# Seven step inputs of a selective state-space recurrence on GpSimd, with their decays in PSUM

## The reference, cut to what matters

```
dt = softplus(dt_low @ dt_proj_w.T + dt_proj_b)          # [B, L, 256]
A  = -exp(A_log)                                         # [256, 16]
def step(h, t):
    dA = exp(dt_t[..., None] * A)                        # decay
    h  = dA * h + (dt_t * u_t)[..., None] * B_t[:, None, :]   # step input
    y_t = einsum('bdn,bn->bd', h, C_t)
y = y + u * D;  y = y * silu(z);  out = (y @ out_proj_w.T) @ fc2_w.T + fc2_b
```

## Time and profile before

| | |
|---|---|
| time, median of 3 runs | 1123.55 us (1122.48 to 1123.56) |
| profiled execution: its time, its span | 1121.12 us, 1119.8 us |
| TensorE busy | 1066.3 us (95%), granted clock 0.991 of full speed |
| VectorE, ScalarE, GpSimd busy | 839.1, 630.4, 763.4 us |
| the recurrence: first to last scan | 790.5 to 1018.9 us |
| the chain that ended last | PE 79%, issue 7%, DVE 6%, POOL 4%, ACT 3% |

### The profile page before, as it was taken

One profiled execution on the slowest core, in us unless ns is written; L12 is line 12 of the kernel. 1 busy time (PEld: TensorE's weight loads), 2 busy tenths in 40 slices (PEclk: granted clock), 3 DMA queues, 4 the chain that ended last, 5 costly groups with the idle time before them and its releaser, 6 DMA issues.

```text
span 1119.8 us, 18526 instructions
## 1 busy us (share of the span) xinstructions
PE 1066.3 (95%) x6860; PEld 662.1 (59%) x6860; DVE 839.1 (75%) x1234; ACT 630.4 (56%) x898; POOL 763.4 (68%) x394
## 2 busy tenths in 40 slices
PE   7999999999999999999999999779789987999998
PEld 4555665665665655665665657767344433446786
DVE  6876976776765775766975748235999999997987
ACT  5554655654644654643554635348986646757663
POOL 5788788787787897877899830230789897994200
PEclk9999999999999999999999999889899999999999
DMA  7000000000000000000000253465565443440000
GB/s 213 1 2 2 1 2 1 2 2 1 2 2 2 1 1 2 2 2 1 6 7 6 77 178 94 136 215 151 182 206 165 143 161 132 147 154 20 10 10 19
DMA packets 55369, 68.91 MB, mean 62 GB/s; under 512 B 23248, under 2 KB 41424, under 8 KB 55280
## 3 DMA queue, kind: packets, MB, share of 16 engines
q1 hardware_dynamic: 52272, 64.65, 18.7%
q0 software_dynamic: 1024, 2.10, 0.6%
q10 hardware_dynamic: 1984, 0.98, 0.3%
HBM read 61.30 MB, written 6.16 MB: 60 GB/s over the span
## 4 chain that ended last, share of the span: by engine, by line
PE 79%; issue 7%; DVE 6%; POOL 4%; ACT 3%; DMA 1%; another core or an unknown queue 1%; POOLq 0%; DVEq 0%; ACTq 0%
PE psum L661 20%; PE psum L622 16%; PE psum L647 6%; PE psum L635 5%; PE psum L1046 3%; PE psum L687 3%; PE psum L952 3%; PE psum L1029 3%; POOL hc L2252 3%; PE psum L746 3%; PE psum L702 2%; PE psum L810 2%; PE psum L821 2%; PE psum L726 2%; PE psum L680 2%
## 5 line engine op out<-in xcount | busy, mean ns | idle before, releaser
L2164 POOL TENSOR_TENSOR psums<-psums,prob 128x1024 f32<-128x1024 f32 x180 | 430.5, 2392 | 26.1 <-POOL psums L2164 0.5
L1627 DVE TENSOR_REDUCE mx<-psum 128x2 f32<-128x1024 f32 x256 | 299.8, 1218 | 102.0 <-PE psum L647 101.6
L1158 ACT ACTIVATE prob<-psum 128x1024 f32<-128x1024 f32 x256 | 261.3, 1026 | 62.6 <-PE psum L635 38.1
L661 PE MATMUL psum<-prob,V 128*64 128x512 f32 x1024 | 238.7, 597 | 0.0
L2252 POOL TENSOR_TENSOR hc<-hs,cc 128x1024 f32<-128x1024 f32 x64 | 151.6, 2368 | 21.1 <-DVE hs L1930 18.6
L1930 DVE TENSOR_TENSOR_SCAN hs<-dA,psum 128x1024 f32<-128x1024 f32 x64 | 146.3, 2287 | 2.2
L661 PEld LDWEIGHTS psum<-prob,V 128*64 128x64 f32 x1024 | 67.7, 137 | 106.7 <-issue 105.0
L2164 POOL TENSOR_TENSOR psums<-prob 128x1024 f32<-128x1024 f32 x30 | 72.1, 2403 | 85.0 <-ACT prob L1158 84.2
L1177 ACT COPY oraw<-psum 128x512 f32<-128x512 f32 x32 | 18.8, 587 | 191.3 <-PE psum L661 191.3
L952 PE MATMUL psum<-hc,ident 128*128 128x512 f32 x256 | 122.5, 601 | 2.8 <-DVE slot_rows_h L1938 1.4
L647 PE MATMUL psum<-k_hi,q_hi 64*128 64x512 f32 x512 | 107.0, 409 | 1.7 <-DVE mx L1627 1.3
(11 more groups left out here) (319 smaller groups left out, 1712.6 us busy)
## 6 DMA issues: line engine op xcount, KB each, us to landing
cc<-C_rows SPq DMA_DIRECT2D x64, 512.0 KB, 3.8
kq_wts<-in_e_rows SPq DMA_DIRECT2D x14, 578.0 KB, 4.2
e_wts<-in_e_rows SPq DMA_DIRECT2D x10, 578.0 KB, 3.9
e_w<-in_e_rows SPq DMA_DIRECT2D x6, 578.0 KB, 5.1
slots_in<-e_zero SPq DMA_DIRECT2D x2, 960.0 KB, 7.1
inv<-sum_rows SPq DMA_DIRECT2D x120, 1.0 KB, 2.0
slots_out<-e_y SPq DMA_DIRECT2D x30, 64.0 KB, 1.8
e_w<-in_e_w SPq DMA_DIRECT2D x1, 1024.0 KB, 7.0
```

Source lines behind the costliest of these rows:

```text
L661: ins = pe.matmul(A.O[HALF[s], :], A.V[pair % 2][:, j, s * DH:(s + 1) * DH], A.prob[unit(pair, c, j) % NPB][:, s * CH:(s + 1) * CH], start ...
L1158: act.activation(A.prob[n % NPB][:, :], slots.bank("score", pair, c, j).rearrange("p s n -> p (s n)"), ACT.Exp, scale=float(DH) ** -0.5).t ...
L1627: dve.tensor_reduce(K.A.mx[:, :, t, c], slots.bank("max", pair, t, c), AXX, ALU.max).then_inc(*slots.inc("max", pair, t, c))
L2164: pool.tensor_tensor(total[:, :], (K.A.prob[(n - 1) % NPB] if j == 1 else total)[:, :], K.A.prob[n % NPB][:, :], ALU.add).then_inc(*K.psum ...
```

## The change

Seven units, 19, 24, 27, 38, 43, 59 and 62 (`POOL_GAINS`), get their step input from GpSimd. For these units:

- SP stores the rows of B beside those of C in DRAM and loads row n of B into all partitions of one of two SBUF buffers (`sp_copy_B`), six units ahead or at unit 15. The buffers are halves of tiles that are free by then: the second half of xrows and of xnT. TensorE spreads no B.
- GpSimd multiplies that buffer by du in place (`pool_gain`), right behind the product of unit u - 3.
- ScalarE writes the decay into the PSUM buffer in which the step input would have stood (`decay_of`). It therefore waits for the scan of unit u - 2, no longer u - 3.
- The scan reads its decay from PSUM and its step input from SBUF.

GpSimd's side work moves: the bias of fc2 for batch 0 goes from unit 21 to ahead of the recurrence; the low parts of w1 stand at units 47, 49, ... 59 instead of 47 to 54; those of w2 at units 60 to 63 and behind the last unit instead of 56 to 63. Three semaphores of GpSimd's clearing at the start are merged into one.

```diff
+W1_LOW = {e: 45 + 2 * e for e in range(1, E1)}
+POOL_GAINS = (19, 24, 27, 38, 43, 59, 62)
+GAIN_AHEAD = 3
+B_FROM = 15
+def copied_at(i):
+    return max(B_FROM, POOL_GAINS[i] - 6, POOL_GAINS[i - 2] + 1 if i >= 2 else 0)
...
     for e in range(E1):
-        one[48 + e - 1] = one.get(48 + e - 1, []) + [("w1hi", e), ("w1lo", e)] * (e > 0)
-        one[56 + e] = [("w2hi", e), ("w2lo", e)]
+        one[48 + e - 1] = one.get(48 + e - 1, []) + [("w1hi", e)] * (e > 0)
+        one[56 + e] = [("w2hi", e)] + [("w2lo", e - 4)] * (e >= 4)
+    for e in range(1, E1):
+        one[W1_LOW[e]] += [("w1lo", e)]
...
+        order += [("w2lo", n + 2)] * (n + 2 < E1)
...
 def pe_spread_B(K, pe, u):
...
+    if u in POOL_GAINS:
+        return
...
+def decay_of(X, u):
+    return X.gain[u % 2] if u in POOL_GAINS else X.dA[u % 3][:, :]
...
 def act_decay(K, act, u):
...
-    if u >= 3:
+    if u in POOL_GAINS:
+        act.wait_ge(X.state_done, u - 1)
+    elif u >= 3:
         act.wait_ge(X.state_done, u - 2)
-    act.activation(X.dA[u % 3][:, :], X.dt[b][:, k, :], ACT.Exp, scale=X.alog[:, k, n:n + 1]).then_inc(X.decay_done, 1)
+    act.activation(decay_of(X, u), X.dt[b][:, k, :], ACT.Exp, scale=X.alog[:, k, n:n + 1]).then_inc(X.decay_done, 1)
...
 def dve_unit(K, dve, u):
...
+    gain = X.gain[u % 2]
+    if u in POOL_GAINS:
+        gain = X.B_copy[POOL_GAINS.index(u) % 2]
+    else:
+        dve.wait_ge(X.B_done, gains_by_dve(u))
...
+        dve.tensor_tensor(gain, gain, (X.du if u else X.dt)[b][:, k, :], ALU.mult).then_inc(X.gain_done, 1)
...
-    dve.tensor_tensor_scan(X.hs[u % 3][:, :], X.dA[u % 3][:, :], X.gain[u % 2], 0.0, ALU.mult, ALU.add).then_inc(X.state_done, 1)
+    dve.tensor_tensor_scan(X.hs[u % 3][:, :], decay_of(X, u), gain, 0.0, ALU.mult, ALU.add).then_inc(X.state_done, 1)
...
+def pool_gain(K, pool, u):
+    X = K.X
+    b, k, n = rec(u)
+    i = POOL_GAINS.index(u)
+    pool.wait_ge(X.du_done, KI * b + k + 1)
+    pool.wait_ge(X.B_copied[i % 2], 16 * (i // 2 + 1))
+    pool.tensor_tensor(X.B_copy[i % 2], X.B_copy[i % 2], X.du[b][:, k, :], ALU.mult).then_inc(X.pool_gained, 1)
...
 def pool_unit(K, pool, u):
...
+    if u + GAIN_AHEAD in POOL_GAINS:
+        pool_gain(K, pool, u + GAIN_AHEAD)
...
-    sp.dma_start(X.C_rows[b, :, :], X.xd[DTR + NS:DTR + 2 * NS, :]).then_inc(X.C_stored, 16)
+    sp.dma_start(X.C_rows[b, :, :], X.xd[DTR:DTR + 2 * NS, :]).then_inc(X.C_stored, 16)
+def sp_copy_B(K, sp, i):
...
+    sp.dma_start(X.B_copy[i % 2], X.C_rows[b, n, :].partition_broadcast(P)).then_inc(X.B_copied[i % 2], 16)
```

More of the change, by code:

```diff
@@ L82, with gains_by_dve, gains_by_pool @@
 SKIP_AT = {1: 14, 2: 11, 3: 11}
+POOL_GAINS = (19, 24, 27, 38, 43, 59, 62)
+GAIN_AHEAD = 3
+B_FROM = 15
+def gains_by_dve(u):
+    return sum(v not in POOL_GAINS for v in range(u + 1))
+def gains_by_pool(u):
+    return sum(v in POOL_GAINS for v in range(u + 1))
+def copied_at(i):
+    return max(B_FROM, POOL_GAINS[i] - 6, POOL_GAINS[i - 2] + 1 if i >= 2 else 0)
 class Signal:
@@ L357, in first_inputs_order @@
     s = NSLOT
-    order = turned(4) + [("down", s + 4), ("fc1", 0), ("fc1_out", 0), ("yrow", s + 4), ("fetch", s + 10)]
+    order = turned(4) + [("down", s + 4), ("fc1", 0), ("fc1_out", 0), ("fc2bias", 0), ("yrow", s + 4), ("fetch", s + 10)]
     order += [("down", s + 5), ("up", s + 6), ("gelu", s + 6), ("inp", 0, 0), ("inp_out", 0, 0), ("yrow", s + 5), ("fetch", s + 11)]
@@ L1635, in dve_cols @@
     if (pair, h) == (0, 0):
-        dve.wait_ge(A.cleared, 7)
+        dve.wait_ge(A.cleared, 8)
     else:
@@ L1917, in dve_unit @@
     b, k, n = rec(u)
[L1918 to L1923, removed]
+    gain = X.gain[u % 2]
[3 more added lines that the diff above has]
+        dve.wait_ge(X.B_done, gains_by_dve(u))
+        if u == 1 or (u and n == 0):
+            dve.wait_ge(X.du_done, KI * b + k + 1)
+        if u == 0:
+            dve.wait_ge(X.dt_done, 1)
+        dve.tensor_tensor(gain, gain, (X.du if u else X.dt)[b][:, k, :], ALU.mult).then_inc(X.gain_done, 1)
     if n == 2 and u > (KI + 1) * NS:
         dve_output(K, dve, *divmod(u // NS - 1, KI))
-    dve.wait_ge(X.gain_done, u + 1)
+    if u in POOL_GAINS:
+        dve.wait_ge(X.pool_gained, gains_by_pool(u))
+    else:
+        dve.wait_ge(X.gain_done, gains_by_dve(u))
     dve.wait_ge(X.decay_done, u + 1)
@@ L2394, in sp_store_C @@
     sp.wait_ge(*K.work.empty("xpj", b, NC - 1))
-    sp.dma_start(X.C_rows[b, :, :], X.xd[DTR + NS:DTR + 2 * NS, :]).then_inc(X.C_stored, 16)
+    sp.dma_start(X.C_rows[b, :, :], X.xd[DTR:DTR + 2 * NS, :]).then_inc(X.C_stored, 16)
+def sp_copy_B(K, sp, i):
+    X = K.X
+    b, k, n = rec(POOL_GAINS[i])
+    sp.wait_ge(X.C_stored, 16 * (b + 1))
+    if i == 0:
+        sp.wait_ge(*K.work.empty("ln", LN_SSM + 1, 1))
+    elif i == 1:
+        sp.wait_ge(*K.work.empty("fc1", 1, 1))
+    else:
+        sp.wait_ge(X.state_done, POOL_GAINS[i - 2] + 1)
+    sp.dma_start(X.B_copy[i % 2], X.C_rows[b, n, :].partition_broadcast(P)).then_inc(X.B_copied[i % 2], 16)
 def sp_spread_C(K, sp, u):
@@ L2414, in sp_unit @@
         sp_spread_C(K, sp, u + NCC - 1)
+    for i in range(len(POOL_GAINS)):
+        if u == copied_at(i):
+            sp_copy_B(K, sp, i)
 def sp_added(K, sp, b, c):
@@ L2477, in two_layer_program @@
         K.first_var, K.first_root = sem("first_variance"), sem("first_root")
-        K.wg_cleared, K.wg_sum, K.wg_root, K.wg_scaled = (sem("wg_" + n) for n in ("cleared", "sum", "root", "scaled"))
+        K.wg_sum, K.wg_root, K.wg_scaled = (sem("wg_" + n) for n in ("sum", "root", "scaled"))
         K.dve_own, K.pool_own = Chain(sem("dve_own")), Chain(sem("pool_own"))
```

51 lines of the change are left out of this document (27 added, 24 removed).

## The result

The changed kernel takes 1128.29 us (median of 5 runs, 1128.03 to 1129.09) against 1122.48 for the kernel before beside it (1121.50 to 1123.56): ratio 1.0054, 95% interval 1.0043 to 1.0066. It is slower, by 5.8 us between the medians, where 1127.2 was forecast (3.7 us slower). The profiled execution of the changed kernel took 1128.03 (span 1126.7).

What follows compares the result with a forecast made beforehand. VectorE paces plain units; TensorE, GpSimd and ScalarE queues bound other stretches. +2.0 at unit 48, +1.3 at the end, +0.4 at the handover: +3.7 on 1121.12 gives 1124.8, plus 2.43 to the median 1127.2; range 1125.5 to 1129.5.

Steps and rivals of the forecast that it cites:

- Units 19, 24, 27: Recurrence up to unit 32: of 3.7 us offered by VectorE, 0.8 arrives, with ends 0 and 1.4.
- GpSimd's walk from the product of unit 16 to the dt of batch 1: 43.5: GpSimd before unit 32: 18 operations and the waits between them take 43.5 us, ending at 895.5 instead of 896.35.
- TensorE's 1.4: TensorE in units 19 to 28: three spreads of B dropped, 3 x 0.46 = 1.4 us, the most that could arrive.
- Unit 43: ScalarE's decay waits for scan 41, so the normed rows start at 942.9, 2.0 us later, and unit 48 at 964.7.
- from there the chain has no gap: From the normed rows to the spread of B for unit 48: their 2.0 us delay carries through to unit 48.
- Units 59, 62: End of the recurrence on GpSimd: product 56 at 995.7, product 63 at 1020.3, 1.3 us later than before.
- Handover: Recurrence to experts: VectorE's low parts of the hidden rows delay GpSimd's last products by 0.4 us (0 to 1.3).
- Prices: Decay into PSUM, 0 to +0.25 us, taken as 0; scan with decay from PSUM, taken unchanged, worst +1.4 seven times.
- Rival 1: ScalarE's queue at unit 43 does not carry through; du bounds unit 48: -0.8 us, 1122.7. Chance 0.17.
- 2: On top of Rival 1, GpSimd keeps up with VectorE at the end: -5.0 us, 1118.5. Chance 0.12.
- 3: VectorE's time is all that counts: -8.7 us, 1114.9. Chance 0.04.
- Rival 4: Worse: a scan or product slowed by the other; over 1129.5, at most +10. Chance 0.05.

Runs made afterwards that it cites:

- experiment 5: The changed kernel with ScalarE's decay of unit 43 moved behind the eight normed rows; ratio 1.0034 to the kernel before.
- experiment 3: The changed kernel without units 59 and 62 on GpSimd; ratio 1.0040 to the kernel before.
- the changed kernel again: The changed kernel, unchanged, run again on another chip for a second trace; ratio 1.0058 to the kernel before.
- experiment 6: The changed kernel with unit 43's decay behind the normed rows and its GpSimd step input behind product 41; ratio 1.0015 to the kernel before.
- experiment 8: The changed kernel without unit 62, w1 low parts back in place, unit 43's decay and step input late; ratio 0.9983 to the kernel before.
- experiment 2: The changed kernel without unit 43 on GpSimd; ratio 1.0018 to the kernel before.
- experiment 4: The changed kernel with extra TensorE matmuls filling the gap before the projection of unit 46; ratio 1.0045 to the kernel before.
- experiment 1: The changed kernel with no step inputs on GpSimd, only the side work moved; ratio 0.9999 to the kernel before.

## Why the prediction was right, and where it was not

The direction, the places and two of the sizes held. The sum was 3.7 and the two traces differ by 6.9. Of the missing 3.2, 1.24 are in normed rows that came later than forecast, 1.67 are TensorE's clock, 0.05 and 0.2 lie at the end. That the time still came within 1.1 us of 1127.2 is in part luck. The forecast added 2.43 to its sum, the distance of the trace of before below its median; the changed kernel's trace lies only 0.26 below its own. Trace against trace, the forecast was 1124.8, its own range 1123.1 to 1127.1, and 1128.03 came.

**Units 19, 24, 27 (said: unit 32 is 0.8 earlier; measured: 0.6 later, 0.57 of it there at unit 12 by chance, so 0.07 from these units).** The failing step is "GpSimd's walk from the product of unit 16 to the dt of batch 1: 43.5". It took 896.98 - 852.59 = 44.39. The rows of GpSimd:

```profile
855.50 2.37 POOL L2286 TENSOR_TENSOR xrows<-xrows,du 128x1024 f32<-128x1024 f32 x1 [0.56 <-DMA xrows<-C_rows]
...
887.06 2.36 POOL L2241 TENSOR_TENSOR xdr<-xd,xdr 64x1024 fp32r<-64x1024 f32 x1 [0.34 <-ACT xdr L1360]
...
896.98 2.36 POOL L2250 TENSOR_TENSOR slotT<-slotT,tmp 128x1024 f32<-128x1024 f32 x1
```

The difference is these two waits, 0.56 + 0.34 = 0.90. The copy of B was given "1 us to spare"; it was priced at the 3.8 of the loads of C, and the copies into xrows took 5.0 in the median. It came late in all nine traces with unit 19, by 0.30 to 0.93. In them GpSimd's first step input starts 19.38 to 20.03 after scan 12, and scan 32 follows it by 49.83 to 49.89 each time: what the copy is late, unit 32 is late. By these rows a copy in time would have brought unit 32 about 0.5 earlier than before; that is an estimate, and no run tried it.

The other wait is this step of GpSimd, here in before:

```profile
886.43 2.35 POOL L2200 TENSOR_TENSOR xdr<-xd,xdr 64x1024 fp32r<-64x1024 f32 x1 [1.78 <-ACT xdr L1334]
```

GpSimd had 1.78 us of idle time there, waiting for ScalarE's cast behind TensorE's projection. I counted GpSimd's instructions as one walk up to dt and passed over a step with a releaser of its own. Counted from scan 12, xdr starts at 51.5 us in the first trace of before and 51.6 in the changed kernel's, and GpSimd's extra products filled most of the idle time ahead of it. TensorE's 1.4 did not bring it forward either, because TensorE had to wait for one of the products that GpSimd had made late, that of unit 18:

```profile
864.88 1.98 PE L978 MATMUL psum<-hc,ident 128*128 128x512 f32 x4 [0.46 <-POOL hc L2303]
```

From there TensorE has no gap up to the projection. In all ten traces with three early units the projection's second half starts 21.53 to 21.56 after product 18 does, and scan 32 stands 21.34 to 21.38 behind it in all fourteen. So the path to unit 32 runs from the copy of B over GpSimd's product 18, TensorE's queue, ScalarE's cast and xdr to du. VectorE is not on it: between scans 12 and 32 it is idle for 4.5 us, where it was idle for 1.2 before.

**Unit 38: right.** 1.27 in every kernel that has it; 1.24 was said.

**Unit 43: the mechanism right, the size not.** The decay starts behind scan 41, the reads of dtp and the rows behind it, ScalarE binds and not the shift (942.45; said 941.1), and the waits for B are at units 46 to 48 (6.1; said 5). The rows start at 944.14 instead of 942.9, because scan 41 ended 0.66 earlier than before and not 2.0: the failed step above and the 0.57 of chance at unit 12. Then the step "from there the chain has no gap", which took TensorE's durations of before: the longer gap that the delay opens ahead of the projection let the clock fall, and the projection, the two spreads of B and the sums behind it took 1.67 more in this trace and 2.56 in the second. The gap was 1.61 in before, with 1.99 for the projection; 2.76, 3.08, 4.24 and 4.47 (experiment 5, the changed kernel, experiment 3, the changed kernel again) go with 2.54, 2.57, 3.78 and 3.78. The earlier gap of 4.69 does not do it by itself: it stands, 4.68 long, in experiments 6 and 8 too, whose projection takes 1.99. Experiments 2, 4, 5 and 6 show both parts. By the Trainium skill (TensorE: Matmul & The Clock Gate, Part 1: The HAM clock gate) the clock is set by how busy TensorE has lately been; the rows agree, with the lower level behind idle 4.69 and 3.08.

**Units 59, 62: right.** Product 56 stands 4.95 + 995.73 = 1000.68 with unit 48 late by 4.95; 995.7 was said. From there to product 63 are 24.64, said 24.6. The 1.35 come back, within 0.02, in all six traces with both units and the moved low parts of w1, and go in experiment 3.

**Handover: the size right (0.6; said 0.4, up to 1.3), the victim wrong.** Products 62 and 63 took 2.39 and 2.38, so GpSimd paid nothing on the path. VectorE did (line 2069 by itself, as the earlier trace rows):

```profile
L2069 DVE TENSOR_TENSOR e_hr_lo<-e_h,e_hr_hi x64: 661/692/4145, 1024.8 to 1121.0; 128x512 fp32r<-128x512 f32 x64
```

The longest, 4.15, is the first: it starts at 1024.79 during a low part of GpSimd (1024.62 to 1025.38), lasts over the whole of product 63 (to 1027.70) and over the low part behind it (to 1028.38), and ends at 1028.93. The gated rows behind it held TensorE 0.37. Of the six traces with a late product 63 four have such an operation of 4.1 and end 101.32 to 101.38 behind the product's start; the two whose longest is 2.7 (experiments 4 and 5) end at 101.19 and 101.17. So about 0.2 of the 0.6 seems to go with its length. The Trainium skill (SBUF — State Buffer, Who interferes with whom) adds that the order of issue decides who blocks, for a whole instruction. The trace fits as to who issued first, but VectorE was held beyond that one instruction, through the two behind it. In experiments 1 and 3 product 63 is not late, the longest is 2115 and 2126 ns, about as before (2126), and nothing is lost.

**Prices: right.** Nothing from 0 to +0.25 for the decay, nothing up to +1.4 for the scan: both came out 0.03 below.

**The rivals.** 1, 2 and 3 are out: ScalarE's queue carried through, GpSimd did not keep up, and VectorE's time alone did not count. Rival 4 is out too: scans took 2.26 and 2.29, products 2.36 to 2.39. Rival 1's step "had the reads been done before the shift, du bounds unit 48" is wrong as well: in experiment 6 the chain over the rows still bound it.
